# Local-attention stack on one core: softmax subtraction moved into sixteen ScalarE exponentials, squares summed in rows, fourth step reordered

## What is computed

```python
q, k, v = split(shift_tokens(x) @ Wqkv)            # heads of 64
q = l2norm(q) * qs ;  k = l2norm(k) * ksc          # a norm for each head and token
q = q*cos*scale + rotate_half(q)*sin*scale         # k with 1/scale
sim = einsum(q, [previous window, own window] of k) * 8.0
sim = where(mask, -max, sim)
x = softmax(sim) @ v @ Wo + x                      # attention
x = (a * gelu(gate)) @ W2 + b2 + x                 # feed-forward, a and gate from layernorm(x) @ W1
```

## Time and profile before

| | |
|---|---|
| device time, median of 3 (lowest, highest) | 4742.06 us (4739.58, 4746.09) |
| profiled execution, and its span | 4749.81 us, 4748.0 us |
| busy: TensorE, VectorE, GpSimd, ScalarE | 93%, 74%, 52%, 52% |
| granted TensorE clock, mean | 0.954 |

### The profile page before, as it was taken

How to read it: one execution, slowest core, us unless ns; L and a number is a source line. 1 busy time by engine, 2 the same in 40 slices (tenths; PEclk the granted TensorE clock), 3 DMA queues, 4 the chain that set the end, 5 groups by cost and what they waited for, 6 DMA issues and landing times. The chain is left out here.

```text
span 4748.0 us, 116556 instructions
## 1 busy us (share of the span) xinstructions
PE 4426.3 (93%) x46020; PEld 2614.7 (55%) x46020; DVE 3530.1 (74%) x3768; ACT 2451.6 (52%) x3764; POOL 2477.3 (52%) x3513
## 2 busy tenths in 40 slices
PE   7999889999999999999999999999999998678898
PEld 3333366666666666666666666666666665322233
DVE  5777478777778778778778778778778776477774
ACT  1666545554555555555455555545555554135564
POOL 1111266666666666666566666666666665122213
PEclk6999989999999999999999999999999999779999
DMA  3222122222222222222222223222222222222220
GB/s 88 56 55 55 55 51 63 57 58 71 63 61 61 55 74 72 53 61 61 73 65 59 57 60 81 57 62 57 57 72 58 58 61 71 42 55 46 48 45 19
DMA packets 182135, 281.98 MB, mean 59 GB/s; under 512 B 58269, under 2 KB 80349, under 8 KB 175965
## 3 DMA queue, kind: packets, MB, share of 16 engines
q1 hardware_dynamic: 154300, 241.72, 21.4%
q10 hardware_dynamic: 27648, 37.79, 3.5%
HBM read 61.77 MB, written 17.56 MB: 17 GB/s over the span
## 5 line engine op out<-in xcount | busy, mean ns | idle before, releaser
L1144 DVE SCALAR_TENSOR_TENSOR x<-l_r,l_qkvec,l_tab 128x1024 f32<-128x1024 f32 x768 | 936.3, 1278 | 31.0 <-ACT l_sq L1047 27.9
L553 DVE TENSOR_REDUCE a_nmax<-a_pair 128x2 f32<-128x1024 f32 x512 | 609.4, 1220 | 223.4 <-PE a_pair L676 223.3
L453 ACT ACTIVATE a_pt<-a_st 128x512 f32<-128x512 f32 x1024 | 543.2, 603 | 281.6 <-PE a_st L660 276.3
L974 POOL TENSOR_TENSOR l_ntmp<-l_seed 128x32 f32<-128x32 f32 (+1 forms) x480 | 112.1, 234 | 777.9 <-ACT l_seed L1030 759.1
L1001 POOL TENSOR_TENSOR l_u<-x 128x512 f32<-128x512 f32 x384 | 491.4, 1280 | 0.0
L1002 POOL TENSOR_TENSOR l_u<-x 128x512 f32<-128x512 f32 x384 | 490.2, 1276 | 0.0
L1317 PE MATMUL l_r<-xs,l_wqkv 128*128 (+1 forms) x768 | 424.6, 660 | 38.8 <-DVEq L1224 38.8
L1406 PE MATMUL l_r<-l_pbd,l_va 128*64 128x160 f32 (+1 forms) x6144 | 441.2, 296 | 18.8 <-DMA l_pbd<-l_pt 18.7
L1007 POOL TENSOR_TENSOR l_p<-l_p,l_srec 128x1024 f32<-128x1024 f32 x192 | 365.4, 1903 | 175.3 <-DVE l_srec L1236 142.0
L1406 PEld LDWEIGHTS l_r<-l_pbd,l_va 128*64 128x64 f32 x6144 | 395.3, 137 | 80.1 <-issue 80.0
L1367 PE MATMUL l_r<-l_kbd,l_qn 64*32 64x128 f32 x24576 | 418.5, 279 | 12.2 <-DMA l_kbd<-l_kn 6.6
(11 more groups left out here) (204 smaller groups left out, 7452.7 us busy)
## 6 DMA issues: line engine op xcount, KB each, us to landing
l_kbd<-l_kn SPq DMA_DIRECT2D x1536, 64.0 KB, 2.0
l_pbd<-l_pt SPq DMA_DIRECT2D x768, 64.0 KB
l_pbd<-l_pt ACTq DMA_DIRECT2D x576, 64.0 KB
a_ks<-a_scr SPq DMA_DIRECT2D x96, 192.0 KB
a_qs<-a_scr SPq DMA_DIRECT2D x288, 64.0 KB
a_scr<-a_parts SPq DMA_DIRECT2D x48, 256.0 KB, 2.5
l_pbd<-l_pt SPq DMA_DIRECT2D x192, 56.0 KB
l_wqkv<-in_wqkv SPq DMA_DIRECT2D x6, 1536.0 KB, 6.5
```

Source lines behind the costliest of these rows:

```text
L453: nc.scalar.activation(pt[n % 2][:, r, :], st[(4 * n + r + par) % 3][:], ACT.Exp, scale=SC).then_inc(exp_done, 1)
L553: nc.vector.tensor_reduce(out=nmax[:, n, 2 * i:2 * i + 2], in_=pair[i][:], op=ALU.max, axis=AX.X, negate=True).then_inc(pair_dve[i], 1)
L1144: last = nc.vector.scalar_tensor_tensor(out=t[a][:, 2 * half:2 * half + 2, :], in0=R[a][:, half, :].unsqueeze(1).to_broadcast([D, 2, T]), ...
```

## The change

In the stack:

- **Softmax.** VectorE no longer subtracts; its maximum is taken negated. ScalarE makes sixteen exponentials of 128x64 straight from PSUM, each with its own column of `smax` as bias, and clears `R[3]` after them and a drain. The factor 8 of the scores is folded into the table for q.
- **Rows of squares.** The sums of squares come out with heads in rows (four groups of 32 partitions, 8 rows used, 128 columns) and not in columns (128x32). TensorE adds the two halves of k's squares itself (8 matmuls) and takes GpSimd's sum for q alone (4 matmuls), so GpSimd makes one addition and not two. What is read, seeded, rooted and cleared is 128 columns wide, not 32. The spread takes 8 matmuls with a 0/1 table from 64 rows each and a wait of TensorE for its own first four; ScalarE's widening copy (L1074) and TensorE's transposes are gone. One more constant of 256 KB is loaded.
- **Order.** VectorE, steps 0 to 2: q's rotation stands ahead of the transpose of the probabilities, and both normalisations ahead of the sum of exponentials. Step 3: the sums of squares come first on TensorE, as in other steps; VectorE reads the norms and rotates q before it waits for the output product; the v projection stands ahead of the variance and waits for the centring.

In the second global attention: the q and k projection comes at step 2 of 16 (before 4), the row maxima of the first half at 10 (before 8), VectorE's splitting one a step at 5 to 9 (before 6, 7, 7, 8, 9), and the load of those rows stands behind the head loads in SyncE's queue.

```diff
-        QK_STEP, ROWS_STEP = (4, 9) if rope is None else (4, 8)
+        QK_STEP, ROWS_STEP = (4, 9) if rope is None else (2, 10)
...
-                if m is not None and rope is not None:
-                    load_rows(0, par)
...
-                if m is not None and rope is None:
+                if m is not None:
                     load_rows(0, par)
...
-                split_slots = (4, 5, 6, 7, 8) if rope is None else (6, 7, 7, 8, 9)
+                split_slots = (4, 5, 6, 7, 8) if rope is None else (5, 6, 7, 8, 9)
...
-                        nc.gpsimd.tensor_tensor(sqs[0][:], sq[0][:, 0, :], sq[0][:, 1, :], ALU.add)
-                        nc.gpsimd.tensor_tensor(sqs[1][:], sq[1][:, 0, :], sq[1][:, 1, :], ALU.add).then_inc(S["sq_sum"], 1)
+                        nc.gpsimd.tensor_tensor(sqs[:], sq[0][:, 0, :], sq[0][:, 1, :], ALU.add).then_inc(S["sq_sum"], 1)
...
-                    if has_ss:
-                        expand()
...
                         act.wait_ge(S["t_ready"], seen.next(S["t_ready"]))
+                        sc = R[3][:].rearrange("p a b -> p (a b)").rearrange("p (u k) -> p u k", k=2 * WIN)
+                        for u_of in range(NT * CH):
+                            last = nc.scalar.activation(p[:, u_of, :], sc[:, u_of, :], ACT.Exp, bias=smax[:, u_of:u_of + 1])
+                        last.then_inc(S["p_ready"], 1)
                         if b is not None:
+                            act.drain()
                             nc.scalar.activation(R[3][:, :, 0:NSS], zeros[:], ACT.Copy).then_inc(S["r3_cleared"], 1)
-                        nc.scalar.activation(p[:], p[:], ACT.Exp, scale=QK_SCALE).then_inc(S["p_ready"], 1)
+                        else:
+                            act.drain().then_inc(S["r3_act"], 1)
...
-                    if c < 3 and has_ss:
+                    if has_ss and c < 3:
                         read_norm()
-                    transpose_p(c)
+                    if c == 3 or b is None:
+                        transpose_p(c)
+                    if has_ss and c == 3:
+                        read_norm()
+                    if c == 3 and b is not None:
+                        rotate(0)
...
                     if b is not None:
-                        rotate(0)
+                        if c < 3:
+                            rotate(0)
+                            transpose_p(c)
                         rotate(1)
...
-                        nc.vector.tensor_reduce(out=smax[:], in_=sc, op=ALU.max, axis=AX.X).then_inc(S["step"], 1)
-                        v.wait_ge(S["step"], seen.next(S["step"]))
-                        nc.vector.tensor_tensor(p[:], sc, smax[:].unsqueeze(2).to_broadcast([D, NT * CH, 2 * WIN]),
-                                                ALU.subtract).then_inc(S["t_ready"], 1)
+                        nc.vector.tensor_reduce(out=smax[:], in_=sc, op=ALU.max, axis=AX.X, negate=True).then_inc(S["t_ready"], 1)
...
                         claim(3)
+                        pe.wait_ge(S["sqk_ready"], seen.next(S["sqk_ready"]))
+                        for half in range(2):
+                            for k in range(NT):
+                                nc.tensor.matmul(R[3][32 * k:32 * k + 2 * CH, 0, 0:D], block8[:, 1, :], sq[1][:, half, 128 * k:128 * k + 128],
+                                                 start=False, stop=False, skip_group_check=True)
                         pe.wait_ge(S["sq_sum"], seen.next(S["sq_sum"]))
                         for k in range(NT):
-                            for a in range(2):
-                                o = (k * 2 + a) * CH
-                                last = nc.tensor.matmul(R[3][:, 0, o:o + CH], sqs[a][:, 128 * k:128 * k + 128], block4[:],
-                                                        start=False, stop=True, skip_group_check=True)
+                            last = nc.tensor.matmul(R[3][32 * k:32 * k + 2 * CH, 0, 0:D], block8[:, 0, :], sqs[:, 128 * k:128 * k + 128],
+                                                    start=False, stop=True, skip_group_check=True)
...
+                    if has_var:
+                        pe.wait_ge(S["centred_pe"], seen.next(S["centred_pe"]))
+                    if b is not None:
+                        project_v()
...
                     if has_ss:
-                        pe.wait_ge(S["rnx_ready"], seen.next(S["rnx_ready"]))
+                        pe.wait_ge(S["rn_ready"], seen.next(S["rn_ready"]))
                         claim(0, "r0_dve_b", "r0_dve_b")
-                        for a in (1, 0):
-                            for k in range(NT):
-                                o = (k * 2 + a) * CH
-                                last = nc.tensor.transpose(R[0][:, 1 - a, 128 * k:128 * k + 128],
-                                                           rnx[:, o:o + CH, :].rearrange("p h i -> p (h i)"), C["ident"][:])
+                        for turn in range(2):
+                            for k in range(2):
+                                for half in range(2):
+                                    rows, a, o = slice(64 * half, 64 * half + 64), (half + turn + 1) % 2, 256 * half + 128 * k
+                                    last = nc.tensor.matmul(R[0][:, 1 - a, o:o + 128], spread8[rows, a, k, :], rn[rows, 0:D], start=True, stop=True)
+                                    if turn == 0:
+                                        last.then_inc(S["b_turn"], 1)
+                            if turn == 0:
+                                pe.wait_ge(S["b_turn"], seen.next(S["b_turn"], 4))
```

More of the change, by code:

```diff
@@ L1334, in body, with project_v @@
                         nc.tensor.matmul(R[2][:, 1, :], C["inv"][:], xs[:, prev, 0:T], start=True, stop=True).then_inc(S["mean_ready"], 1)
-                    if c == 3 and has_ss:
-                        sums_of_squares()
-                    if has_var:
-                        if not has_ss:
-                            claim(3)
-                        pe.wait_ge(S["fsq_ready"], seen.next(S["fsq_ready"]))
-                        for k in range(NT):
-                            last = nc.tensor.matmul(R[3][:, 1, k:k + 1], fsq[:, 128 * k:128 * k + 128], C["inv"][:, 0:1],
-                                                    start=(b is None), stop=True, skip_group_check=True)
-                        last.then_inc(S["var_ready"], 1)
-                        due[3] = due[3] + ["normv_read"]
-                    if b is not None:
+                    def project_v():
                         if c == 0:
@@ L1356, in body @@
                         last.then_inc(S["v_act"], 1)
+                    if has_var:
+                        pe.wait_ge(S["centred_pe"], seen.next(S["centred_pe"]))
+                    if b is not None:
+                        project_v()
+                    if has_var:
+                        if not has_ss:
+                            claim(3)
+                        pe.wait_ge(S["fsq_ready"], seen.next(S["fsq_ready"]))
+                        for k in range(NT):
+                            last = nc.tensor.matmul(R[3][:, 1, k:k + 1], fsq[:, 128 * k:128 * k + 128], C["inv"][:, 0:1],
+                                                    start=(b is None), stop=True, skip_group_check=True)
+                        last.then_inc(S["var_ready"], 1)
+                        due[3] = due[3] + ["normv_read"]
                     if live(c, 2, b, prev):
-                        claim(3, "r3_cleared" if b is not None else "r3_dve")
+                        claim(3, "r3_cleared" if b is not None else "r3_act")
                         pe.wait_ge(S["qn_ready"], seen.next(S["qn_ready"]))
@@ L1685, in layouts @@
     inv = (np.float32(1.0) / scale).astype(np.float32)
[L1686 removed]
+    a["tab"] = np.stack([np.tile((m * f).T, (CH, 1)) for f in (scale * np.float32(QK_SCALE), inv) for m in (cos, sin)], axis=1)
     i, j = np.arange(D)[:, None] % WIN, np.arange(2 * WIN)[None, :]
```

61 lines of the change are left out of this document (27 added, 34 removed).

## The result

The changed kernel takes 4999.15 us (median of 4, 4985.87 to 5008.51), the kernel before in the same comparison 4743.43 (4739.58 to 4746.09). The ratio is 1.0538, 95% interval 1.0507 to 1.0568: slower by 5.4%. The profiled execution took 4985.87 us, the shortest of the four; its span is 4984.1.

The account below looks back on a forecast made before the run. VectorE's closed ring was taken to bound steps 0 to 2, with TensorE some tenths below. 2 x 1.0 + 1.65 + 1.8 = 5.4 us a body, +260 over 48 bodies, -2 for the second attention: median 5000, range 4800 to 5170.

Parts of the forecast that it names:

- The forecast case: Stack: sixteen exponentials and the later clear lengthen the chain, as does the fourth step's order; 5000 us, chance 0.72.
- sums take: TensorE's sums of squares after the clear: 24 records on four column tiles, 0.82 us, bounds 0.6 and 1.95.
- step 0 to 1: Maximum of step 0 to that of step 1: 14.3 us, +1.0, and the same for step 1 to 2.
- The price of an exponential: ScalarE's softmax: starts 0.23 us apart, bounds 0.16 and 0.31, so sixteen take 3.8 us where one took 1.04.
- a sign of being right: ScalarE's softmax in steps 0 to 2: sixteen exponentials in 3.5 to 4.1 us.
- the next wait: Products with v, behind the moved transpose's transfers: end at +4.9 us, ahead of the clear at +5.6; limiting if exponentials were cheap.
- signature of "wrong": Steps 0 to 2 released by the banded DMA, one of the signs named against the forecast.
- The fourth step: Step 3's new order and its neighbours: step 2 to 3 +1.65 us, step 3 to 0 +1.8; the spread about 1.25.
- The clean body: Four undisturbed steps of a stack body, 69.8 us before: claimed to grow 5.4 us, +260 over 48 bodies.
- The 1.3 us a body carried unchanged: Part of the 71.1 us body beyond the 69.8 of undisturbed steps, taken to stay as it was.
- The clock rival: TensorE's 2.5 us pauses a step lower its clock for a fifth of the time: +190, 5190 us, chance 0.08.
- The second attention: Second global attention: moving projection, split and rows reshuffles waits on `pair[1]`; -2 us, bounds -11 and +11.

Follow-up runs that it names:

- e5: Changed kernel with the second half of k's squares left out of TensorE's sums, 4 matmuls fewer a step: 4954.81 us, ratio 1.0431.
- e12: Changed kernel with unused TensorE matmuls added, one ahead of step 3's scores and one ahead of the products with v in steps 0 and 1: 4919.12 us.
- e7: Kernel before with only the softmax part: no subtraction, sixteen exponentials, then drain and clear; 4901 us was expected, 5020.69 us measured.
- e9: Kernel before with the sixteen exponentials alone, plus two unused matmuls ahead of the sums of squares in steps 1 and 2: 4945.59 us.
- e11: Changed kernel with one unused matmul added on TensorE ahead of the scores in step 3: 4984.57 us, ratio 1.0490.
- e4: Changed kernel with the old softmax and VectorE's whole old order in steps 0 to 2 put back: 4833.01 us, ratio 1.0179.
- e8: Kernel before with the second attention's edits and softmax split by PSUM bank: eight biased exponentials for the first, subtraction and one exponential for the second: 4703.97 us.
- e2: Changed kernel with the old softmax alone put back (subtraction on VectorE, clear, one exponential): 4959.29 us, ratio 1.0452.
- e3: Changed kernel with the transpose of the probabilities again ahead of q's rotation in steps 0 to 2: 4966.66 us, ratio 1.0471.
- e1: Kernel before with only the second global attention's four edits: 4725.5 us, ratio 0.9951.

## Why the prediction was right, and where its terms were not

The forecast case came: slower, by the chain that the prediction wrote out. Its steps, in us from the maximum's start, against the timelines above:

| | predicted | measured |
|---|---|---|
| products with v: start, end | 2.7, 4.9 | 2.75, 5.04 |
| sixteen exponentials take | 3.8 | 3.38 |
| clear of `R[3]` done | 5.56 | 5.11 |
| sums take | 0.82 | 0.77 |
| q's rotation starts | 8.3 | 7.85 |
| step 0 to 1 | 14.3 | 13.9 |
| step 2 to 3: sums start | 7.9 | 8.64 |
| step 2 to 3: residual, variance, scores | 13.7, 19.0, 21.5 | 13.74, 19.11, 21.65 |
| step 2 to 3 in all | 24.75 | 24.96 |
| step 3 to 0: output copy, sums | 5.5, 12.85 | 5.04, 12.77 |
| step 3 to 0 in all | 21.9 | 21.72 |

- **The price of an exponential** was mis-sized. Sixteen in 3.38 us, one of 0.36, put the starts (3.38 - 0.36) / 15 = 0.20 us apart, where the prediction took 0.23 and named 3.5 to 4.1 us for all sixteen as a sign of being right. The rule of the Trainium skill that it weighed (page ScalarE: Activation LUTs, section What ACT_TABLE_LOAD costs) has 280 ns plus 0.833 ns a column, 333 ns for one: the trace has 362. Its overlap of about 93 ns isn't what the trace shows, which is 362 - 200, about 160. So the clear is done 0.45 us earlier than predicted, and both short steps grew by 0.57 us and not 1.0.
- **The wait beside it.** The prediction called the products with v the next wait were exponentials cheaper. They end 0.07 us ahead of the clear's end: with the exponentials 0.1 us faster, the transfer would have set the step. Its signature of "wrong", steps 0 to 2 released by the banded transfer, is half there: the idle time stands ahead of L1412, yet the sums go as the clear ends.
- **The fourth step** held: +1.87 measured on the clean step against +1.65, +1.64 against +1.8. The spread takes 1.52 us and not 1.25; in the clean step it still runs when the next maximum starts (1391.55 and 1392.32), so it isn't ahead of it.
- **The clean body** is thus 74.4 us against 69.8, +4.6 and not +5.4: 47 x 4.6 = 217.
- **Instruction fetches** were not foreseen, +42 us in twelve bodies. The prediction named no rival of the kind. The change has 3,072 TensorE records more in all, 64 a body, and e5, with 32 of them fewer, has none of the extra fetches.
- **The 1.3 us a body carried unchanged** held in size: 76.54 - 74.41 is 2.13, less 0.90 for the fetches is 1.23. What it holds was not asked. In e12 the mean body is 75.09, 0.66 over the clean value, 0.3 of it fetches: most of the 1.23 was the lower clock, and e7, e9 and e11 show that it moves from place to place. The kernel before carries it as well: 16 of its 48 steps 0 to 1 have a mean granted clock under 0.97, the change has 8. No run fills the pauses of the kernel before.
- **The clock rival** got 0.08 and a price of 190 us. In the change it isn't the cause, since the stack's mean granted clock is 0.98 before and after; in e7 it makes what lies above the expected 4901 in large part, as e9 took 75 of those 120 us back. The rival was priced on the right mechanism and dismissed for slack on TensorE, and what holds it off in the change wasn't tried by itself; a difference that its rows show is that the products with v lie in the middle of the pause there.
- **The second attention** was mis-sized: -19 us where the prediction took -2 within -11 to +11. It bounded the gain by TensorE's wait on `pair[1]` and did not look at GpSimd's 75.5 us for the projection.

The sum: +217 clean, +42 fetches, -4 for the rest, -19 attention, 236 us of span. The prediction had 260 - 2 = 258. That its 5000 lies 1 us from the median is luck in good part. Its clean chain was 43 us too dear, and the fetches that it left out cost 42; its attention was 17 us off, which the choice of execution hides: the profiled execution, predicted at 5008, took 4985.87, and it lies 13 us below the median of its kernel where that of before lay 7.7 above.

The parts come out as follows. Softmax with VectorE's order cost 3.0 us a body (e4 against the change), rows of squares with the fourth step and the fetches 2.4 (e4 against before). Neither of the two parts is a gain. They don't simply add up: the exponentials alone, in the old order, cost 5.1 us a body (e7).

## What to carry to other kernels

Moving work from a full engine to a half idle one pays only if it doesn't lengthen the chain that turns both. Here one pass of 1.2 us on VectorE became sixteen starts of 0.20 on ScalarE, ahead of the clear that lets TensorE go on; cutting the work by bank so that both engines run at once (e8) was the form that helped. Of an order and a mechanism that belong together, undo both before judging either (e2 and e3 gave 40 and 32 us, e4 with both 166). And price a new pause of TensorE twice, once for its length and once for the clock behind it: where a wait can't be removed, spare products in it can be faster than none (e9, e12).

## What the chip showed that was not expected

- **The clock behind pauses.** Products behind pauses of 1.5 to 1.9 us took 3.44 for 2.02, 3.95 for 2.29 and 2.85 for 1.96 us, in stretches of granted clock 0.56 to 0.68; in the kernel before one behind a pause of 0.39 us took 2.07 for 1.12. The same pause brings the lower level in some bodies and not in others, so its length alone doesn't decide. One pause of a body filled moved the slow place to another pause (e11, 15 us less in the median); pauses filled in three of the four steps ended it (e12, granted clock 1.00).
- **Where the slow stretch falls.** In e7 it is not the work right behind the pause but that after it: the sums run at 1.00, the projections behind them at 0.68 and 0.66.
- **Instruction fetches.** The change has 233 packets where the kernel before, e1, e7 and e8 have 116; the extra ones fall on two layers of six and cost 3.5 us in each of twelve bodies there on average. e12 has still more instructions and 178 packets, in one layer, so the number of instructions alone doesn't tell.
